# State products added up in memory by GpSimd transfers, and the weight stages' lower parts subtracted on GpSimd

## The chip, the core and the metric

The kernel runs on one core of one Trainium2 chip. The metric is the device time of one execution in microseconds (us). The core's engines work side by side, each through its own list of instructions in order, and wait for each other through semaphores: TensorE (PE, with weight loads as PEld), VectorE (DVE), ScalarE (ACT), GpSimd (POOL) and SyncE (SP), which here only issues transfers. Matrix results are in PSUM banks of 128 x 512 float32.

## What is computed

A decoder layer of three parts, each with a residual and a layer norm: differential attention, a state-space scan over a context, and a mixture of 16 experts. The change touches the first two, which one loop computes together.

```python
q, k, v = split(hidden @ Wqkv.T + b)                 # 16 q heads and 8 k heads of 128, v in pairs
p = softmax(q1 k1) - lam * softmax(q2 k2)            # causal
o = (p @ v) * rms * subln_w * (1 - LAMBDA_INIT)
x = layernorm(x + o.reshape(B, S, 2048) @ out_w.T + out_b)
...
def step(state, inp):                                # 4 batches, 512 channels, 16 states, 512 steps
    d, b, c, u = inp
    state = state * exp(d * A) + (d * u) * b
    return state, einsum('bdn,bn->bd', state, c)     # sum over the 16 states
y = (y + D * u) * silu(x)
```

## The kernel before

Matrix products are made from split operands: a value is a high part (rounded to the fp32r type) and a lower part (the value less the high part), and `three` (L602) issues three products hi*hi, hi*lo, lo*hi. So each weight and each result is cut in two: ScalarE writes the high part, and another engine subtracts for the lower part.

The main loop, `attend_and_scan`, has 64 passes p (and 2 that drain it) on each engine, in an order written out by hand. Each pass has two halves. In it the attention's work for one block m of 128 rows and one group g of heads goes through TensorE: scores of two units, turns of the probabilities, two projections (`project`, which run 7 ahead of their pass by AHEAD), values, turned heads, and `project_out(p-2)`. Sixteen passes are one group g, and there are 4 groups; four passes are one batch of a group. The x operand of the projections is reloaded from memory every four passes (`load_x`, L713 to L715) into the one buffer that there is.

Beside it runs the scan: in each pass one of 64 states (4 batches x 16), in two halves of 128 x 1024. For half k, k = 0 to 127: GpSimd's `drive(k)` writes dt*u*B into a slot of the ring `st` (4 slots); ScalarE's `decay` and VectorE's `scan` run twice over it; GpSimd then gates it (times C, L1279) and adds it into `y_sb` (L1284), and does `drive(k + 3)`. After a batch's 16 states, two transfers on GpSimd's own queue add `y_sb` to `scratch_y` in memory (L1291). So GpSimd has three operations in each half pass, and k is also the number of the half pass.

Weights come in stages of 128 x 512, 12 for each group: 8 of Wqkv (c = 0 to 7, called W stages here) and 4 of out_w (c = 8 to 11, called out stages). SP loads one into one of two slots of `w_stage`; `stage_high` on ScalarE writes the high part with the factor (the score scale, or the subln column) put on; `stage_low` on VectorE computes stage * factor - high. SP loads stage n + 2 into the slot when stage_lo says that stage n is done (L619), in its place in SP's list. `W_AT` places the W stages of the next group at half passes 19 to 24, 26 and 27 of a group. Two out stages are at the end of pass p % 16 == 1, before `proj_high` and the scan there, and two in the first half of pass p % 16 == 2, before the scan there. TensorE waits for them in two places: `project` (L769) and the first `project_out` of a group (L844), which comes in the first half of pass p % 16 == 2, just behind the scores.

When the loop is over, the expert phase begins: GpSimd adds `outb` to the first x (L1616), VectorE takes statistics of that and adds the last attention block (L1153) behind them, ScalarE waits for this block's transfer and for the scan's last sums.

Of the kernel before, what the change touches and what calls it, by code (L numbers as in the profile page):

```python
# [21 lines left out]
ALU = mybir.AluOpType  # L22
# [478 lines left out]
NB = 2  # L501
NSTAGE = 12
# [34 lines left out]
def attend_and_scan(nc, d, s, ctx, place, banks, early):  # L537
# [35 lines left out]
    y = sb("y_sb", [P, CT, T])  # L573
# [7 lines left out]
    def proj_bank(r):  # L581
# [7 lines left out]
             "stage_hi", "stage_lo", "vb_loaded", "vb_hi", "vb_lo", "xa_loaded", "xb_loaded",  # L589
# [4 lines left out]
             "dt_loaded0", "dt_loaded1", "dtu_loaded0", "dtu_loaded1", "y_added0", "y_added1",  # L594
             "b_loaded0", "b_loaded1", "c_loaded0", "c_loaded1",
             "dA_done", "dbu_done", "scan_done", "gated", "piece_done")
# [14 lines left out]
    def half(buf, h):  # L611
        return buf[:, 2 * h:2 * h + 2, :].rearrange("p c t -> p (c t)")

# [72 lines left out]
    def sync(sp, F):  # L686
# [65 lines left out]
        for h in range(2):  # L752
            sp.wait_ge(S[f"acc_stored{h}"], 16 * NM // 2)
            sp.wait_ge(S[f"y_added{h}"], 16 * B)
# [125 lines left out]
    def scalar(act, F, stages=None, blocks=()):  # L880
        def stage_high(n):

            g, c = divmod(n, NSTAGE)
            act.wait_ge(S[f"stage_loaded{n % 2}"], 16 * (n // 2 + 1))
            if c < 8:
                if g > 0:
                    act.wait_ge(S["proj_done"], 8 * (4 * g - 1) + (1, 1, 2, 3, 4, 5, 7, 7)[c] + 1)
                nc.scalar.activation(w[0][:, :, TILE_COL[c]:TILE_COL[c] + HD],
                                     stage[:, n % 2, :].rearrange("p (k n) -> p k n", k=KT), ACT.Copy,
                                     scale=SCALE if 2 <= c < 6 else 1.0).then_inc(S["stage_hi"], 1)  # L890
            else:
                t = c - 8
                act.wait_ge(S["subln_scaled"], 1)
# [161 lines left out]
    def vector(dve, F, stages=None, blocks=()):  # L1055
        def stage_low(n):

            g, c = divmod(n, NSTAGE)
            dve.wait_ge(S["stage_hi"], n + 1)
            raw = stage[:, n % 2, :]  # L1060
            if c < 8:
                cut = slice(TILE_COL[c], TILE_COL[c] + HD)
                nc.vector.scalar_tensor_tensor(w[1][:, :, cut], raw.rearrange("p (k n) -> p k n", k=KT),
                                               SCALE if 2 <= c < 6 else 1.0, f32(w[0][:, :, cut]),
                                               ALU.mult, ALU.subtract).then_inc(S["stage_lo"], 1)
            else:
                t = c - 8
                nc.vector.scalar_tensor_tensor(ow[1][:, t, :], raw, subln[:, t % 2:t % 2 + 1],
# [112 lines left out]
        for p in range(NM + 2):  # L1181
# [9 lines left out]
            if 2 * p in W_AT:  # L1191
                stage_low(W_AT[2 * p])
# [1011 lines left out]
```

## Time and profile before

| | |
|---|---|
| median of 3 runs | 1639.57 us (1638.88 to 1640.35) |
| the profiled execution | 1641.0 us, with a span of 1638.9 us |
| busy: PE, DVE, ACT, POOL | 1425.3, 1304.8, 1044.7, 1232.5 us |
| main loop | about 178 to 1149 us of the span |
| transfers, hardware queue (SP's) | 188.36 MB |
| transfers, GpSimd's queue | 4.19 MB |

The profile shows one execution. A row of the timeline has an instruction's start, its duration, its place in the code, tiles, and in brackets the idle time of its engine just before it and the instruction that ended it. The duration of one that stands behind another on the same engine can hold some waiting for that other, so the distance between two starts tells the pace. PEclk is the granted share of TensorE's full clock: 1.00 is 2.4 GHz and 0.50 is 1.2 GHz.

### The profile page before, as it was taken

How to read it: one execution, taken by the hardware profiler on the slowest of the kernel's cores; microseconds unless marked ns; L12 is line 12 of the kernel's file. 1: busy time of each engine (PE TensorE's matmuls, PEld its weight loads, DVE VectorE, ACT ScalarE, POOL GpSimd, SP SyncE). 2: the span in 40 equal slices, each digit the busy share in tenths (PEclk: the TensorE clock that was granted, in tenths of full speed). 3: DMA queues.
4: the chain of work that ended last, by engine and by line, in shares of the span. 5: the costliest groups of instructions: out<-in, count | busy, mean ns of one | idle time of the engine just before them, and what ended most of it. 6: DMA issues, size and time to landing. Idle time of an engine off the chain costs nothing.

```text
span 1638.9 us, 23260 instructions
## 1 busy us (share of the span) xinstructions
PE 1425.3 (87%) x7632; PEld 1145.2 (70%) x7632; DVE 1304.8 (80%) x2375; ACT 1044.7 (64%) x2407; POOL 1232.5 (75%) x613
## 2 busy tenths in 40 slices
PE   4646799999999999999999999986478999998996
PEld 1213678877888887888887788875366676676784
DVE  4998688899888899888899889886638668487575
ACT  3887557666666666666666566664457657577474
POOL 1346489999899999899999899999567347176263
PEclk8767889999999999999999999999699999998998
DMA  5484433453642443632453532325352032121021
GB/s 174 161 293 184 161 95 106 129 152 101 188 124 87 136 146 124 174 112 83 142 155 117 173 116 78 126 76 155 96 155 75 23 101 78 41 79 65 27 71 58
DMA packets 121664, 194.03 MB, mean 118 GB/s; under 512 B 10740, under 2 KB 60408, under 8 KB 120008
## 3 DMA queue, kind: packets, MB, share of 16 engines
q1 hardware_dynamic: 120392, 188.36, 35.7%
q0 software_dynamic: 1152, 4.19, 1.5%
q8 instruction: 60, 0.98, 0.2%
q14 instruction: 60, 0.49, 0.1%
HBM read 145.99 MB, written 46.53 MB: 117 GB/s over the span
## 4 chain that ended last, share of the span: by engine, by line
PE 41%; DVE 20%; POOL 16%; issue 12%; ACT 6%; DMA 2%; SPq 0%; POOLq 0%; DVEq 0%; ACTq 0%
PE banks L604 10%; PE banks L605 9%; PE banks L606 9%; POOL act_buf L1939 6%; DVE state L1160 4%; POOL state L1279 3%; POOL state L1253 3%; PE banks L1481 2%; PE banks L1482 2%; PE banks L1483 2%; DVE banks L1997 1%; PE banks L814 1%; POOL x_work L1616 1%; DVE banks L452 1%; DVE negmax L1100 1%
## 5 line engine op out<-in xcount | busy, mean ns | idle before, releaser
L1279 POOL TENSOR_TENSOR state<-state,Cn 128x1024 f32<-128x1024 f32 x120 | 292.6, 2438 | 47.8 <-DVE state L1160 47.5
L1160 DVE TENSOR_TENSOR_SCAN state<-banks,state 128x512 f32<-128x512 f32 x256 | 310.9, 1214 | 4.7 <-ACT banks L984 2.2
L1253 POOL TENSOR_TENSOR state<-dtu_sb,Bn 128x1024 f32<-128x1024 f32 x128 | 311.1, 2431 | 1.5 <-DMA Bn<-scratch_bc 1.4
L1939 POOL TENSOR_TENSOR act_buf<-act_buf,wb 128x512 f32<-128x512 f32 x128 | 165.8, 1297 | 172.5 <-ACT act_buf L1839 170.5
L1284 POOL TENSOR_TENSOR y_sb<-y_sb,state 128x1024 f32<-128x1024 f32 x120 | 287.2, 2393 | 9.4
L984 ACT ACTIVATE banks<-dt_sb,negA 128x512 f32<-128x512 f32 x256 | 177.4, 693 | 106.7 <-DVE state L1160 105.8
L604 PE MATMUL banks<-x_hi,w_hi 128*128 128x512 f32 (+1 forms) x512 | 189.4, 370 | 31.6 <-DVE qT_lo L1090 14.7
L606 PE MATMUL banks<-x_hi,w_lo 128*128 128x512 f32 (+1 forms) x512 | 179.4, 350 | 0.0
L605 PE MATMUL banks<-x_lo,w_hi 128*128 128x512 f32 (+1 forms) x512 | 179.2, 350 | 0.0
L604 PEld LDWEIGHTS banks<-x_hi,w_hi 128*128 128x128 f32 x512 | 101.7, 199 | 51.9 <-DVE qT_lo L1090 18.7
L1987 DVE TENSOR_TENSOR hid_lo<-banks,hid_hi 128x512 fp32r<-128x512 f32 x136 | 93.7, 689 | 53.9 <-ACT hid_hi L1851 51.8
L1997 DVE TENSOR_TENSOR banks<-banks,act_buf 128x512 f32<-128x512 f32 x136 | 94.4, 694 | 49.3 <-POOL act_buf L1939 25.6
L1100 DVE TENSOR_REDUCE negmax<-banks 128x2 f32<-128x512 f32 (+3 forms) x128 | 103.8, 811 | 20.1 <-PE banks L806 20.1
L1851 ACT CAST hid_hi<-banks 128x512 fp32r<-128x512 f32 x136 | 79.4, 584 | 61.3 <-DVE banks L1997 49.8
L606 PEld LDWEIGHTS banks<-x_hi,w_lo 128*128 128x128 f32 x512 | 101.6, 198 | 12.3
L605 PEld LDWEIGHTS banks<-x_lo,w_hi 128*128 128x128 f32 x512 | 102.2, 200 | 9.2
L604 PE MATMUL banks<-ow_hi,hT_hi 128*128 128x512 f32 x256 | 106.2, 415 | 1.5 <-DVE hT_lo L1146 1.4
L1481 PE MATMUL banks<-xl_hi,cw_hi 128*128 128x512 f32 x256 | 102.4, 400 | 3.0 <-ACT act_buf L1837 2.9
L930 ACT ACTIVATE prob<-banks,negmax 128x256 f32<-128x256 f32 (+3 forms) x128 | 67.4, 527 | 57.3 <-DVE negmax L1100 55.7
L1837 ACT ACTIVATE act_buf<-banks 128x512 f32<-128x512 f32 x136 | 81.6, 600 | 33.0 <-PE banks L1483 27.9
L1482 PE MATMUL banks<-xl_lo,cw_hi 128*128 128x512 f32 x256 | 101.5, 397 | 0.0
L1483 PE MATMUL banks<-xl_hi,cw_lo 128*128 128x512 f32 x256 | 101.5, 397 | 0.0
(219 smaller groups left out, 4448.9 us busy)
## 6 DMA issues: line engine op xcount, KB each, us to landing
x_hi<-scratch_xs SPq DMA_DIRECT2D x32, 512.0 KB, 5.0
x_lo<-scratch_xs SPq DMA_DIRECT2D x32, 512.0 KB, 6.3
Cn<-scratch_bc SPq DMA_DIRECT2D x64, 256.0 KB, 3.4
Bn<-scratch_bc SPq DMA_DIRECT2D x64, 256.0 KB, 3.9
scratch_acc<-acc_sb SPq DMA_DIRECT2D x64, 256.0 KB, 2.1
wb<-scratch_wT SPq DMA_DIRECT2D x64, 256.0 KB, 3.2
acc_sb<-scratch_acc SPq DMA_DIRECT2D x48, 256.0 KB, 3.1
w_stage<-in_w SPq DMA_DIRECT2D x32, 256.0 KB, 3.3
```

The lines of the kernel that those rows point to most:

```text
L604: nc.tensor.matmul(out, at_l(lhs[0]), at_r(rhs[0]), start=start, stop=False)
L605: nc.tensor.matmul(out, at_l(lhs[0]), at_r(rhs[1]), start=False, stop=False)
L606: return nc.tensor.matmul(out, at_l(lhs[1]), at_r(rhs[0]), start=False, stop=stop)
L984: nc.scalar.activation(dA[:, :], dt[:, ct, :], ACT.Exp, scale=s["negA"][:, ct * NS + state:ct * NS + state + 1]) \
L1160: nc.vector.tensor_tensor_scan(row, dA[:, :], row, 0.0, ALU.mult, ALU.add) \
L1253: nc.gpsimd.tensor_tensor(st[:, k % 4], dtu[:, 2 * h:2 * h + 2, :], Bn[:, state % NB, :].unsqueeze(1).broadcast_to([P, 2, T]), ALU.mult).t ...
L1279: nc.gpsimd.tensor_tensor(to, st[:, k % 4], Cn[:, state % NB, :].unsqueeze(1).broadcast_to([P, 2, T]), ALU.mult).then_inc(S["gated"], 1)
L1284: nc.gpsimd.tensor_tensor(y[:, 2 * h:2 * h + 2, :], y[:, 2 * h:2 * h + 2, :], st[:, k % 4], ALU.add).then_inc(S["piece_done"], 1)
L1481: nc.tensor.matmul(out, at_l(lhs[0]), at_r(rhs[0]), start=start, stop=False)
L1482: nc.tensor.matmul(out, at_l(lhs[0]), at_r(rhs[1]), start=False, stop=False)
L1483: return nc.tensor.matmul(out, at_l(lhs[1]), at_r(rhs[0]), start=False, stop=stop)
L1939: nc.gpsimd.tensor_tensor(act_[:, N % 3, :], act_[:, N % 3, :], wb[:, E % 3, :], ALU.mult) \
```

## The change

The sum y in on-chip memory and its adds are gone. Each gated half state, 128 x 1024, is itself added to `scratch_y` by a transfer on GpSimd's queue: 128 of them, where there were 8. Two transfers to the same half of y must not be in flight together, so each waits for the one two half passes earlier, and the ring has 6 slots, so that a slot is free again when its transfer has landed. The `stage_low` of the first 8 stages stays on VectorE; the 40 others go to GpSimd, as a plain subtraction. For that, ScalarE first scales the stage in its slot, waits for itself, and then writes the high part: two operations for each of these 40 stages, where there was one. The places in ScalarE's list are the old ones. On GpSimd they follow the gate and the drive of the same half pass.

```diff
@@ attend_and_scan
-    y = sb("y_sb", [P, CT, T])
+    st_more = sb("state_more", [P, 2, 2, T])
+    def ring(k):
+        at = k % RING
+        return st[:, at] if at < 4 else st_more[:, at - 4]
+
+    def stage_scale(c):
+        return SCALE if 2 <= c < 6 else 1.0 if c < 8 else subln[:, c % 2:c % 2 + 1]
@@ scalar: stage_high
             act.wait_ge(S[f"stage_loaded{n % 2}"], 16 * (n // 2 + 1))
+            raw = stage[:, n % 2, :]
+            if n >= 8:
+                act.wait_ge(S["subln_scaled"], 1)
+                nc.scalar.activation(raw, raw, ACT.Copy,
+                                     scale=stage_scale(c)).then_inc(S["stage_scaled"], 1)
+                act.wait_ge(S["stage_scaled"], n - 7)
...
-                nc.scalar.activation(ow[0][:, t, :], stage[:, n % 2, :], ACT.Copy,
-                                     scale=subln[:, t % 2:t % 2 + 1]).then_inc(S["stage_hi"], 1)
+                nc.scalar.activation(ow[0][:, t, :], raw, ACT.Copy).then_inc(S["stage_hi"], 1)
@@ vector: the loop
-            if 2 * p in W_AT:
-                stage_low(W_AT[2 * p])
-            if p % 16 == 2 and p < NM:
-                stage_low(NSTAGE * (p // 16) + 10)
-                stage_low(NSTAGE * (p // 16) + 11)
...
-            if p % 16 == 1 and p < NM:
-                stage_low(NSTAGE * (p // 16) + 8)
-                stage_low(NSTAGE * (p // 16) + 9)
...
-            if 2 * p + 1 in W_AT:
-                stage_low(W_AT[2 * p + 1])
@@ gpsimd
+        def wait_added(k):
+            state, h = divmod(k, 2)
+            pool.wait_ge(S[f"y_added{h}{state % 2}"], 16 * (state // 2 + 1))
@@ gpsimd: drive
+            if k >= RING:
+                wait_added(k - RING)
+            nc.gpsimd.tensor_tensor(ring(k), dtu[:, 2 * h:2 * h + 2, :],
                                     Bn[:, state % NB, :].unsqueeze(1).broadcast_to([P, 2, T]),
                                     ALU.mult).then_inc(S["dbu_done"], 1)
@@ gpsimd: new
+        def stage_low(n):
+            g, c = divmod(n, NSTAGE)
+            if n == 8:
+                pool.wait_ge(S["stage_lo"], 8)
+            pool.wait_ge(S["stage_hi"], n + 1)
+            raw = stage[:, n % 2, :]
+            if c < 8:
+                cut = slice(TILE_COL[c], TILE_COL[c] + HD)
+                nc.gpsimd.tensor_tensor(w[1][:, :, cut], raw.rearrange("p (k n) -> p k n", k=KT),
+                                        f32(w[0][:, :, cut]), ALU.subtract).then_inc(S["stage_lo"], 1)
+            else:
+                nc.gpsimd.tensor_tensor(ow[1][:, c - 8, :], raw, f32(ow[0][:, c - 8, :]), ALU.subtract) \
+                    .then_inc(S["stage_lo"], 1)
@@ gpsimd: the loop
+            nc.gpsimd.tensor_tensor(ring(k), ring(k),
                                     Cn[:, state % NB, :].unsqueeze(1).broadcast_to([P, 2, T]),
                                     ALU.mult).then_inc(S["gated"], 1)
-            if r > 0:
-                pool.wait_ge(S["gated"], k + 1)
-                nc.gpsimd.tensor_tensor(y[:, 2 * h:2 * h + 2, :], y[:, 2 * h:2 * h + 2, :],
-                                        st[:, k % 4], ALU.add).then_inc(S["piece_done"], 1)
             if k + 3 < NDRIVE:
                 drive(k + 3)
-            if r == NS - 1:
-                pool.wait_ge(S["piece_done"], added(k))
-                nc.gpsimd.dma_start(d["y"][b][:, 2 * h * T:2 * (h + 1) * T], half(y, h), accum_op=ALU.add) \
-                    .then_inc(S[f"y_added{h}"], 16)
+            if k in W_AT:
+                stage_low(W_AT[k])
+            if k % 32 in (3, 4):
+                for c in range(2):
+                    stage_low(NSTAGE * (k // 32) + 2 * (k % 32 + 1) + c)
+            pool.wait_ge(S["gated"], k + 1)
+            if r > 0:
+                wait_added(k - 2)
+            nc.gpsimd.dma_start(d["y"][b][:, 2 * h * T:2 * (h + 1) * T],
+                                ring(k).rearrange("p c t -> p (c t)"), accum_op=ALU.add) \
+                .then_inc(S[f"y_added{h}{state % 2}"], 16)
```

The expert phase's waits for y_added are spread over the four new semaphores in the same way.

GpSimd's list at half passes 35 and 36 (pass 17's second half and pass 18's first, where the second group's out stages are), before:

```order
L1279 TENSOR_TENSOR state<-state,Cn 128x1024 [waits c_loaded1,scan_done]
L1284 TENSOR_TENSOR y_sb<-y_sb,state 128x1024 [waits gated]
L1253 TENSOR_TENSOR state<-dtu_sb,Bn 128x1024 [waits piece_done,b_loaded1]
L1279 TENSOR_TENSOR state<-state,Cn 128x1024 [waits c_loaded0,scan_done]
L1284 TENSOR_TENSOR y_sb<-y_sb,state 128x1024 [waits gated]
L1253 TENSOR_TENSOR state<-dtu_sb,Bn 128x1024 [waits piece_done,b_loaded1]
```

The same two half passes on GpSimd now:

```order
L1283 TENSOR_TENSOR state_more<-state_more,Cn 128x1024 [waits c_loaded1,scan_done]
L1248 TENSOR_TENSOR state<-dtu_sb,Bn 128x1024 [waits y_added00,b_loaded1]
L1264 TENSOR_TENSOR ow_lo<-w_stage,ow_hi 128x512 [waits stage_hi] x2
L1296 DMA scratch_y<-state_more 128x1024 [waits y_added10,gated]
L1283 TENSOR_TENSOR state<-state,Cn 128x1024 [waits c_loaded0,scan_done]
L1248 TENSOR_TENSOR state<-dtu_sb,Bn 128x1024 [waits y_added10,b_loaded1]
L1264 TENSOR_TENSOR ow_lo<-w_stage,ow_hi 128x512 [waits stage_hi] x2
```

The add has gone, a transfer stands last, and the four subtractions of the out stages stand behind gate and drive; the second pair is behind the gate that waits for pass 18's second scan.

VectorE's list in the same place, from the end of pass 17 to the second scan of pass 18 (qT_lo is a projection's lower part, L1160 the scan), before:

```order
L1121 TENSOR_TENSOR pT_lo<-banks,pT_hi 128x384 [waits pt_hi]
L1068 SCALAR_TENSOR_TENSOR ow_lo<-w_stage,subln,ow_hi 128x512 [waits stage_hi] x2
L1160 SCALAR_TENSOR_TENSOR state<-banks,state 128x512 [waits dbu_done,dA_done]
L1090 SCALAR_TENSOR_TENSOR qT_lo<-banks,qk_bias,qT_hi 128x512 [waits proj_hi]
L1146 TENSOR_TENSOR hT_lo<-banks,hT_hi 128x512 [waits ot_hi]
L1100 TENSOR_REDUCE negmax<-banks 128x2 [waits scores_done]
L1121 TENSOR_TENSOR pT_lo<-banks,pT_hi 128x384 [waits pt_hi]
L1160 SCALAR_TENSOR_TENSOR state<-banks,state 128x512 [waits dbu_done,dA_done]
...
L1090 SCALAR_TENSOR_TENSOR qT_lo<-banks,qk_bias,qT_hi 128x512 [waits proj_hi]
L1068 SCALAR_TENSOR_TENSOR ow_lo<-w_stage,subln,ow_hi 128x512 [waits stage_hi] x2
L1160 SCALAR_TENSOR_TENSOR state<-banks,state 128x512 [waits dbu_done,dA_done]
```

On VectorE the two rows of L1068 are gone now and nothing takes their place, so each scan follows the row above it.

## Rows read from the trace of the kernel before

**Rows 1.** Windows: stretch, its length, busy time (count) of each engine, PEclk, DMA

```profile
980.00:1090.00 110.00, 109.96 (x696) 94.42 (x696) 94.28 (x187) 72.70 (x203) 108.69 (x47) 1.00 0.30 97
320.00:430.00 110.00, 104.55 (x629) 88.41 (x628) 101.20 (x183) 71.14 (x200) 103.89 (x45) 0.97 0.48 144
```

**Rows 2.** Timeline, VectorE: one attention block's add of four passes

```profile
322.35 0.68 DVE L1153 TENSOR_TENSOR acc_sb<-banks,acc_sb 128x512 f32<-128x512 f32 x1
...
415.35 0.68 DVE L1153 TENSOR_TENSOR acc_sb<-banks,acc_sb 128x512 f32<-128x512 f32 x1
...
993.12 0.68 DVE L1153 TENSOR_TENSOR acc_sb<-banks,acc_sb 128x512 f32<-128x512 f32 x1
...
1076.99 0.68 DVE L1153 TENSOR_TENSOR acc_sb<-banks,acc_sb 128x512 f32<-128x512 f32 x1
```

**Rows 3.** Timelines of VectorE and TensorE around the second group's out stages

```profile
446.74 2.56 DVE L1068 SCALAR_TENSOR_TENSOR ow_lo<-w_stage,subln,ow_hi 128x512 fp32r<-128x512 f32 x1 [0.33 <-ACT ow_hi L896]
451.79 0.80 PE L604 MATMUL banks<-x_hi,w_hi 128*128 128x512 f32 x1 [3.50 <-DVE qT_lo L1090]
458.70 1.40 DVE L1068 SCALAR_TENSOR_TENSOR ow_lo<-w_stage,subln,ow_hi 128x512 fp32r<-128x512 f32 x2
460.02 1.22 DVE L1160 TENSOR_TENSOR_SCAN state<-banks,state 128x512 f32<-128x512 f32 x1
460.25 0.47 PE L604 MATMUL banks<-ow_hi,hT_hi 128*128 128x512 f32 x1
```

**Rows 4.** Windows, as rows 1: behind TensorE's wait of 3.50 us

```profile
452.00:456.00 4.00, 4.00 (x10) 3.13 (x11) 2.93 (x7) 1.72 (x6) 3.92 (x3) 0.50 0.52 164
```

**Rows 5.** The tile w_stage: ScalarE's instructions, durations ns min/median/max, first and last start

```profile
L888 ACT ACTIVATE w_hi<-w_stage x32: 613/632/651, 22.9 to 872.3; 128x512 fp32r<-128x512 f32 x32
...
L896 ACT ACTIVATE ow_hi<-w_stage,subln x16: 710/715/722, 203.2 to 943.3; 128x512 fp32r<-128x512 f32 x16
```

**Rows 6.** Timeline, GpSimd: the loop's last half passes and what follows them

```profile
1125.60 2.34 POOL L1279 TENSOR_TENSOR state<-state,Cn 128x1024 f32<-128x1024 f32 x1
1128.02 2.35 POOL L1284 TENSOR_TENSOR y_sb<-y_sb,state 128x1024 f32<-128x1024 f32 x1
1130.33 2.36 POOL L1279 TENSOR_TENSOR state<-state,Cn 128x1024 f32<-128x1024 f32 x1
...
1135.45 0.88 POOL L1291 DMA_DIRECT2D scratch_y<-y_sb  x1 [0.30 <-POOL y_sb L1284]
1136.07 2.68 POOL L1279 TENSOR_TENSOR state<-state,Cn 128x1024 f32<-128x1024 f32 x1
...
1142.08 5.23 POOL L1616 TENSOR_TENSOR x_work<-x_work,outb 128x512 f32<-128x512 f32 x4
```

**Rows 7.** Timelines of VectorE, SP and TensorE: the x load in a W stage

```profile
354.31 1.21 DVE L1160 TENSOR_TENSOR_SCAN state<-banks,state 128x512 f32<-128x512 f32 x1
...
359.33 0.63 SPq L637 DMA_DIRECT2D x_lo<-scratch_xs  x1
...
368.29 0.37 PE L604 MATMUL banks<-x_hi,w_hi 128*128 128x256 f32 x1
```

**Rows 8.** The tile x_lo between 355 and 363 us: landing of its two loads

```profile
DMA to landing us min/median/max: 6.6/6.9/7.2
```

**Rows 9.** Timelines of VectorE and TensorE, end of the loop

```profile
1125.74 1.22 DVE L1160 TENSOR_TENSOR_SCAN state<-banks,state 128x512 f32<-128x512 f32 x1 [1.88 <-POOL state L1253]
...
1139.96 0.69 DVE L1146 TENSOR_TENSOR hT_lo<-banks,hT_hi 128x512 fp32r<-128x512 f32 x1 [1.44 <-ACT hT_hi L975]
1143.70 0.69 DVE L1582 BATCH_NORM_STATS2 stats<-x_work 128x6 f32<-128x512 f32 x1 [3.04 <-POOL x_work L1616]
...
1148.43 0.69 DVE L1153 TENSOR_TENSOR acc_sb<-banks,acc_sb 128x512 f32<-128x512 f32 x1
```

**Rows 10.** The page's queues (packets, MB, share of 16 engines) and issues (count, KB, landing us)

```profile
q0 software_dynamic: 1152, 4.19, 1.5%
...
scratch_y<-y_sb POOLq DMA_DIRECT2D x8, 512.0 KB, 6.9
```

More of the change, by code:

```diff
@@ L501 @@
 NB = 2
+RING = 6
 NSTAGE = 12
@@ L593, in attend_and_scan @@
              "acc_loaded0", "acc_loaded1", "acc_stored0", "acc_stored1",
-             "dt_loaded0", "dt_loaded1", "dtu_loaded0", "dtu_loaded1", "y_added0", "y_added1",
+             "dt_loaded0", "dt_loaded1", "dtu_loaded0", "dtu_loaded1", "y_added00", "y_added01", "y_added10", "y_added11",
              "b_loaded0", "b_loaded1", "c_loaded0", "c_loaded1",
-             "dA_done", "dbu_done", "scan_done", "gated", "piece_done")
+             "dA_done", "dbu_done", "scan_done", "gated")
     S = {n: ctx.enter_context(nc.semaphore(n)) for n in names}
@@ L753, in sync @@
             sp.wait_ge(S[f"acc_stored{h}"], 16 * NM // 2)
-            sp.wait_ge(S[f"y_added{h}"], 16 * B)
+            for odd in range(2):
+                sp.wait_ge(S[f"y_added{h}{odd}"], 16 * NSTATE // 2)
     def tensor(pe, F, blocks=None):
@@ L888, in stage_high @@
                 nc.scalar.activation(w[0][:, :, TILE_COL[c]:TILE_COL[c] + HD],
-                                     stage[:, n % 2, :].rearrange("p (k n) -> p k n", k=KT), ACT.Copy,
-                                     scale=SCALE if 2 <= c < 6 else 1.0).then_inc(S["stage_hi"], 1)
+                                     raw.rearrange("p (k n) -> p k n", k=KT), ACT.Copy,
+                                     scale=stage_scale(c) if n < 8 else 1.0).then_inc(S["stage_hi"], 1)
             else:
                 t = c - 8
-                act.wait_ge(S["subln_scaled"], 1)
                 if g > 0:
                     act.wait_ge(S["out_done"], 16 * g)
-                nc.scalar.activation(ow[0][:, t, :], stage[:, n % 2, :], ACT.Copy,
-                                     scale=subln[:, t % 2:t % 2 + 1]).then_inc(S["stage_hi"], 1)
+                nc.scalar.activation(ow[0][:, t, :], raw, ACT.Copy).then_inc(S["stage_hi"], 1)
         def vb_high(g):
@@ L1056, in stage_low @@
         def stage_low(n):
-            g, c = divmod(n, NSTAGE)
             dve.wait_ge(S["stage_hi"], n + 1)
[L1060 to L1068, printed above, removed]
-                                               f32(ow[0][:, t, :]), ALU.mult, ALU.subtract) \
-                    .then_inc(S["stage_lo"], 1)
+            cut = slice(TILE_COL[n], TILE_COL[n] + HD)
+            nc.vector.scalar_tensor_tensor(w[1][:, :, cut], stage[:, n % 2, :].rearrange("p (k n) -> p k n", k=KT),
+                                           stage_scale(n), f32(w[0][:, :, cut]),
+                                           ALU.mult, ALU.subtract).then_inc(S["stage_lo"], 1)
         def vb_low(g):
@@ L1158, in scan @@
             dve.wait_ge(S["dbu_done"], i // 2 + 1)
-            row = st[:, i // 2 % 4, i % 2, :]
+            row = ring(i // 2)[:, i % 2, :]
             nc.vector.tensor_tensor_scan(row, dA[:, :], row, 0.0, ALU.mult, ALU.add) \
@@ L1677, in first_loads @@
         for h in range(2):
-            sp.wait_ge(A[f"y_added{h}"], 16)
+            for odd in range(2):
+                sp.wait_ge(A[f"y_added{h}{odd}"], 16 * NS // 2)
         load_y(sp, 0)
@@ L1868, in scalar @@
         for n in range(2):
-            act.wait_ge(A[f"y_added{n}"], 16 * B)
+            for odd in range(2):
+                act.wait_ge(A[f"y_added{n}{odd}"], 16 * NSTATE // 2)
         for n in range(2):
```

16 lines of the change are left out of this document (1 added, 15 removed).

## The prediction

> **What bounds the kernel now.** I read the windows first. In plain passes (980 to 1090 us) TensorE is busy for 109.96 of 110 us at full clock, and GpSimd for 108.69 [rows 1]. So both are full, and the question is who ends last. In the passes with W stages (320 to 430 us) TensorE is busy for 104.55 of 110 at a granted clock of 0.97, so something makes it wait. The distance of attention blocks says how much that is: the same six passes take 83.87 us in a plain place (993.12 to 1076.99) and 93.00 us with the W stages of the second group in them (322.35 to 415.35) [rows 2]. I take this excess of 9.1 us for each of the three times that W stages are loaded in the loop, 27 us.
>
> The timelines tell its cause: VectorE. The first of the out stages' lower parts takes 2.56 us on it, where two together take 1.40 us at 458.70, while GpSimd happens to be idle. Scan, projection and heads queue up behind, and TensorE waits 3.50 us, until 451.79 [rows 3]. After that its granted clock is 0.50 (1.2 GHz), with 10 matmuls in 4 us [rows 4], so about 0.40 us each, of which full clock would give back 0.20.
>
> GpSimd is nearly full, but it holds up little: only at the loop's end does VectorE's scan wait for it (1.88 us at 1125.74) [rows 9]. Its three operations of a half pass cost 2.42 + 2.31 us and as much as the latter for the drive (1125.60, 1128.02, 1130.33), 7.1 us in all [rows 6], beside 83.87 / 12 = 7.0 us that TensorE needs here. **So taking 2.4 us from GpSimd frees an engine that is not last in most of the loop**. What the change can win is the 27 us of the W stages, a like stall at the out stages, and the loop's end.
>
> **GpSimd's new half pass.** The add goes (120 times). A transfer comes: at 1135.45 it starts 0.30 us after the add's end, and the next gate, 2.68 instead of some 2.4 us long, has really begun at about 1136.35, so it costs 1.2 us of GpSimd [rows 6]. Gate 2.35, drive 2.35 and transfer 1.2 make 5.9 us. A lower part of 128x512 on GpSimd is like L1616, 5.23 / 4 = 1.3 us [rows 6]: 7.2 us in a half pass with a W stage. That is the pace of TensorE, so GpSimd keeps up, now with slack in plain passes. The wait for the transfer of two half passes earlier is 14 us behind it, and such a transfer lands in 6.9 us [rows 10]: nothing. A ring of 6 is wide enough for the same reason.
>
> **ScalarE** does one operation more for 40 stages, 0.63 to 0.72 us [rows 5], plus some 0.15 us of waiting for itself. At W stages it lies mostly in waits of ScalarE for VectorE, which was late there; I leave 0.5 us a group for it. At the out stages two of them stand before `proj_high`, for which TensorE waits: 1.65 us.
>
> **Out stages, the main cost.** There are four such places, one a group. At the end of pass 17 VectorE loses 3.14 us of lower parts (446.74 to 449.88, when the scan behind them starts) and ScalarE adds 1.65 us, so TensorE restarts about 1.4 us earlier than 451.79. But the second pair is in pass 18. Before, it stood on VectorE before the second scan, was done at 460.02, and TensorE began the group's first `project_out` at 460.25 with hardly a wait [rows 3]. Now it stands on GpSimd behind gate(36) and drive(39), and gate(36) waits for that very scan. The scan starts at 460.02 - 1.32 (the pair in front of it) - 1.4 - some 0.5 (the half clock after a shorter wait is shorter) = 456.8 and ends 1.1 later, 457.9. Then 0.1 + 2.35 + 2.35 + 2 x 1.3 = 7.4 us make 465.3. **TensorE, with nothing to do since about 458, starts `project_out` at 465.4 in place of 460.25, 5.1 us later.** It comes out of a wait of 7 us, so its 12 matmuls run at half clock, 12 x 0.20 = 2.4 us more. Everything behind is bound by TensorE, so nothing is given back. A group costs 7.5 us, four cost **+30.0 us**. Bounds: 3.5 a group (no clock loss, GpSimd early by 1.5) to 9.5 (the loads of the pair, which wait for the first pair on GpSimd, late by 2): +14 to +38.
>
> **W stages.** The 9.1 us go with VectorE's lower parts, but a new wait comes. SP's list has, in pass 11's second half, the load of a stage that waits for the lower part of half pass 23, and behind it the load of x for the projections of pass 12. Before, x_lo was issued at 359.33, 3.9 us after pass 11's last scan had ended (354.31 + 1.13), and was used at 368.29, 12.9 us after it [rows 7]. With GpSimd about 1.0 us behind, gate 2.4, drive 2.35 and lower part 1.3 end 7.05 us after the scan; a stage, an acc and the x_hi load go before, 1.9 us; x_lo is issued at 9.0 and lands 6.6 to 7.2 us later [rows 8], at 15.9. TensorE waits 3.0 to 3.4 us and pays half clock for some 1.8 more. With ScalarE's 0.5 and VectorE's v bias part, which stays (0.5), 6.2 of 9.1 us are left: 2.9 x 3 = **-8.7 us**. Bounds: 0 to -27, from a wait as long as the old one to none.
>
> **The end.** The scan's wait of 1.88 us goes. The last hT_lo, at 1139.96, comes to 1138.1. The statistics waited for GpSimd's x_work, which began at 1142.08 after the last transfer; GpSimd is now through with its loop some 9 us earlier (last gate and transfer, 3.6 us after the last scan), so they start at 1138.8 and take 3.7 us of work. The last block's add comes at 1142.5 instead of 1148.43 [rows 9]: **-5.9 us** (-4 to -8).
>
> **Sum.** 30.0 - 8.7 - 5.9 = +15.4 us. On the profiled execution's 1641.0 us this is 1656.4; the median of the runs is 1.4 below, so 1655.0.
>
> **A page that speaks against the change.** The transfer's issue is priced at 1.2 us by the row at 1135.45, where VectorE was not in such an operation. The Trainium skill, SBUF — State Buffer, section SBUF: two separate sides, says that GpSimd cannot write a transfer's descriptors while VectorE runs an operation in a two-port mode. No row here shows it; the third rival has it as a mechanism.
>
> **Rivals.** *First, not slower:* the x load comes in time and the out stages cost only their 5.1 us. The point is whether x_lo lands within 12.9 us of the scan, so is issued by 6. For it speaks that SP's queue was in time before by 2.1 us; against it, the 7.05 us to the lower part, each of which is a row. It gives -27 - 5.9 + 20.4 = -12.5: 1627.1 us. If there is also no clock loss and the lower parts come early, 1620.
>
> *Second, transfers in each other's way.* Eight such transfers took 1.5% of the span of all 16 engines [rows 10], 3.1 us each, 128 take 0.43 of the loop on top of the 0.30 to 0.48 there [rows 1]. If each of the 15 x loads lands 3.1 us later, it is 1.0 us past its use by the margin there [rows 7, 8], and with 1.5 us of half clock this is 15 x 2.5 = 38 us more: 1693. Against it: the margin is greater in plain passes, and the queues are not full on average. The Trainium skill, DMA: Bandwidth & Descriptors, section Issuing engines are not separate DMA queues, says that all queues share the 16 engines; its sum for a transfer of this size would be 3.2 us, where the row has 6.9.
>
> *Third, GpSimd stays the bound*, because a transfer costs it more than the row says while VectorE works. From 2.3 us a transfer on, its half pass is longer than TensorE's 7.0; at 2.6 it is 0.3 x 128 = 38 us in place of the W stages' gain, 1680 to 1700. Then the change doesn't do what it says.
>
> **Chances.** Forecast 0.50, first rival 0.25, second 0.13, third 0.12. What a measurement can't tell from no change is 0.2%, 3.3 us. Of the forecast 0.05 lies within it, and of the first rival 0.05; the rest of the first, 0.20, is faster, all else, 0.70, slower. The forecast's own range is 1641 to 1672. 8 times in 10 the time should be between 1625 and 1686, which takes in most of the first rival and the lower part of the last two.
>
> **What would show it.** Right: TensorE's first `project_out` of each group, four times, behind a wait of 6 to 9 us that ends on GpSimd's ow_lo, and a PEclk of 0.50 after it; the wait of 3.50 us down to about 2; the x matmuls of passes 12, 28 and 44 behind a wait for a transfer; VectorE's last L1153 about 6 us nearer to its last scan; GpSimd under 88% busy in plain passes, whose six passes still take 84 us. Wrong: no wait at `project_out`; plain passes longer than 84 us (second or third rival, told apart by GpSimd's busy share); no wait for x (first).

## The result and the profile after

The changed kernel takes 1718.24 us (median of 4 runs, 1710.75 to 1726.39), the kernel before 1639.64: a ratio of 1.048, interval 1.045 to 1.050. It is slower by 78.6 us where the prediction had 15.4, outside its range of 1625 to 1686. The profiled execution was the longest of the four; its span of 1724.6 us is 85.7 more than the 1638.9 of before, and the sums below are made against that.

The same two spans of six passes as in [rows 2], then windows (stretch, length, busy time and count of each engine, PEclk, DMA share, GB/s) of a plain place and of the second group's W stages, as [rows 1]:

```profile
330.40 0.68 DVE L1159 TENSOR_TENSOR acc_sb<-banks,acc_sb 128x512 f32<-128x512 f32 x1
...
434.63 0.68 DVE L1159 TENSOR_TENSOR acc_sb<-banks,acc_sb 128x512 f32<-128x512 f32 x1
...
1079.02 0.68 DVE L1159 TENSOR_TENSOR acc_sb<-banks,acc_sb 128x512 f32<-128x512 f32 x1
...
1162.91 0.68 DVE L1159 TENSOR_TENSOR acc_sb<-banks,acc_sb 128x512 f32<-128x512 f32 x1
```

```profile
1070.00:1150.00 80.00, 79.96 (x501) 68.89 (x499) 70.41 (x145) 54.11 (x155) 62.91 (x34) 1.00 0.81 175
340.00:450.00 110.00, 92.53 (x556) 78.56 (x554) 77.64 (x159) 66.34 (x183) 74.31 (x43) 0.92 0.67 171
```

Plain passes are what they were: 83.89 us for six, TensorE full, GpSimd down from 99% to 79% busy, although the DMA engines are now busy for 0.81 in place of 0.30. The six passes with W stages take 104.2 in place of 93.0 us. So the loss is in places. TensorE's longest waits between 200 and 1180 us (us in total, times, longest) are of three kinds:

```profile
PE banks L605 <- issue: 42.7, 3, 15.5
PE banks L605 <- POOL ow_lo L1264: 30.6, 4, 8.3
PE banks L605 <- DMA x_lo<-scratch_xs: 18.6, 3, 9.9
```

Where the view names "issue", it shows no releaser; these three are the first x matmuls of passes 12, 28 and 44, and each starts within 0.2 us of the landing of x_lo, so I read them as waits for x.

To sum the losses I take the distances of the blocks' adds (L1159, numbered from 0) less those in plain places (14.67, 15.48, 14.45, 12.29 us for number mod 4 = 1, 2, 3, 0). The sum of this **excess** over the places, with what lies behind the loop, is the whole difference. In the first group the out stages come before block 0's add, so there the later start of this add counts as theirs (6.5 us):

| place, blocks | before | after | difference | predicted |
|---|---|---|---|---|
| W stages, 8 to 13, 24 to 29, 40 to 45 | 26.5 | 59.1 | +32.6 | -8.7 |
| batch change, 15, 31, 47 | 0.0 | 25.8 | +25.8 | not in the sum |
| out stages, four groups | | | +27.4 | +30.0 |
| end of the loop, 58 to 63 | -15.4 | -17.3 | -1.9 | -5.9 |
| behind the loop | | | +1.7 | 0 |

The batch change is the pass at which the scan goes to its next batch and SyncE loads new halves of dt and dtu, three times in the loop.

**W stages.** Pass 11's last scan on VectorE and the first x matmul of pass 12 on TensorE, then SyncE's DMAs and GpSimd around them, in the W stages of the second group (start, length, idle before and what ended it):

```profile
360.01 1.21 DVE L1166 TENSOR_TENSOR_SCAN state_more<-banks,state_more 128x512 f32<-128x512 f32 x1
...
390.10 0.55 PE L605 MATMUL banks<-x_hi,w_hi 128*128 128x256 f32 x1 [15.54 <-issue]
```

```profile
365.85 0.55 SPq L630 DMA_DIRECT2D w_stage<-in_w  x1
366.44 0.62 SPq L659 DMA_DIRECT2D Cn<-scratch_bc  x1
367.10 0.48 SPq L705 DMA_DIRECT2D scratch_acc<-acc_sb  x1
367.63 0.90 SPq L654 DMA_DIRECT2D Bn<-scratch_bc  x1
379.89 0.55 SPq L630 DMA_DIRECT2D w_stage<-in_w  x1
380.48 0.62 SPq L700 DMA_DIRECT2D acc_sb<-in_x  x1
381.14 0.53 SPq L645 DMA_DIRECT2D x_hi<-scratch_xs  x1
381.72 0.89 SPq L645 DMA_DIRECT2D x_lo<-scratch_xs  x1
```

```profile
355.39 2.39 POOL L1248 TENSOR_TENSOR state<-dtu_sb,Bn 128x1024 f32<-128x1024 f32 x1 [5.35 <-DMA Bn<-scratch_bc]
357.75 1.29 POOL L1261 TENSOR_TENSOR w_lo<-w_stage,w_hi 128x512 fp32r<-128x512 f32 x1
...
364.28 1.54 POOL L1261 TENSOR_TENSOR w_lo<-w_stage,w_hi 128x512 fp32r<-128x512 f32 x1
365.51 1.15 POOL L1296 DMA_DIRECT2D scratch_y<-state_more  x1
366.12 2.95 POOL L1283 TENSOR_TENSOR state_more<-state_more,Cn 128x1024 f32<-128x1024 f32 x1
376.30 2.35 POOL L1248 TENSOR_TENSOR state<-dtu_sb,Bn 128x1024 f32<-128x1024 f32 x1 [7.23 <-DMA Bn<-scratch_bc]
378.60 1.26 POOL L1261 TENSOR_TENSOR w_lo<-w_stage,w_hi 128x512 fp32r<-128x512 f32 x1
```

The scan ended at 361.22. The x_lo load is issued at 381.72, 20.5 us later, where the prediction had 9.0 and before 3.8 [rows 7]. Read the rows as a ring. GpSimd's drive waits for B (7.23 us at 376.30). B was issued at 367.63, because it stands in SyncE's list behind the stage load of 365.85, which waited for the lower part that ends at 365.8. And this lower part stands on GpSimd behind a drive that had waited for B (5.35 us at 355.39). The next stage load, at 379.89, waits for the lower part of 378.60, and x stands behind it. So two half passes take some 20 us (355.39 to 376.30, drive to drive) in place of 14.

**Batch change.** SyncE, pass 13 to 16, with the last line of TensorE:

```profile
433.41 0.47 SPq L649 DMA_DIRECT2D dt_sb<-scratch_dt  x1
...
434.45 0.43 SPq L649 DMA_DIRECT2D dtu_sb<-scratch_dtu  x1
434.93 0.43 SPq L649 DMA_DIRECT2D dt_sb<-scratch_dt  x1
435.40 0.43 SPq L705 DMA_DIRECT2D scratch_acc<-acc_sb  x1
435.88 0.59 SPq L654 DMA_DIRECT2D Bn<-scratch_bc  x1
447.88 0.33 SPq L700 DMA_DIRECT2D acc_sb<-in_x  x1
448.26 0.53 SPq L645 DMA_DIRECT2D x_hi<-scratch_xs  x1
```

```profile
459.50 0.55 PE L605 MATMUL banks<-x_hi,w_hi 128*128 128x256 f32 x1 [9.86 <-DMA x_lo<-scratch_xs]
```

The acc load waits until the acc store of the same parity (issued at 435.40) has landed: 12.5 us, behind three loads of 512 KB that came together. In the kernel before these three were issued at 408.44, 410.18 and 414.46, and the store landed in 3.0 us.

**Out stages.** As predicted. GpSimd and TensorE in pass 18, where there was hardly a wait before [rows 3], and a window behind:

```profile
488.21 2.64 POOL L1283 TENSOR_TENSOR state<-state,Cn 128x1024 f32<-128x1024 f32 x1
490.51 2.62 POOL L1248 TENSOR_TENSOR state<-dtu_sb,Bn 128x1024 f32<-128x1024 f32 x1
492.81 2.75 POOL L1264 TENSOR_TENSOR ow_lo<-w_stage,ow_hi 128x512 fp32r<-128x512 f32 x2
```

```profile
495.71 0.77 PE L605 MATMUL banks<-ow_hi,hT_hi 128*128 128x512 f32 x1 [8.27 <-POOL ow_lo L1264]
```

```profile
496.00:499.00 3.00, 3.00 (x8) 2.33 (x8) 1.65 (x8) 0.85 (x2) 0.40 (x1) 0.50 0.76 83
```

Gate, drive and two lower parts, then TensorE at half clock: four such waits, 7.7 us on average. The wait of 3.50 us for the projection [rows 3] is down to 1.73.

### The profile page after: what moved, and what is told of

Same layout as the page of the kernel before. It is cut to its first block, busy times and chain, and to the rows that moved or that the text cites. A ratio compares the mean times of both kernels' runs of the same rounds, so it can differ in the third digit from the quotient of the medians.

```text
span 1724.6 us, 23458 instructions
## 1 busy us (share of the span) xinstructions
PE 1437.6 (83%) x7632; PEld 1156.0 (67%) x7632; DVE 1247.8 (72%) x2335; ACT 1067.4 (62%) x2447; POOL 1092.3 (63%) x653
## 4 chain that ended last, share of the span: by engine, by line
PE 28%; issue 25%; POOL 22%; DVE 11%; DMA 7%; ACT 4%; SPq 1%; POOLq 0%; DVEq 0%; ACTq 0%
PE banks L605 6%; PE banks L606 5%; PE banks L607 5%; POOL state L1283 5%; POOL act_buf L1947 5%; POOL scratch_y L1296 3%; DMA Bn<-scratch_bc 2%; PE banks L1487 2%; POOL state_more L1283 2%; PE banks L1488 2%; PE banks L1489 2%; DMA w_stage<-in_w 2%; POOL state L1248 1%; DMA scratch_acc<-acc_sb 1%; DVE banks L2005 1%
## 5 line engine op out<-in xcount | busy, mean ns | idle before, releaser
L1248 POOL TENSOR_TENSOR state<-dtu_sb,Bn 128x1024 f32<-128x1024 f32 x86 | 215.6, 2508 | 128.6 <-DMA Bn<-scratch_bc 117.7
L1283 POOL TENSOR_TENSOR state<-state,Cn 128x1024 f32<-128x1024 f32 x86 | 228.1, 2653 | 70.3 <-DVE state L1166 65.6
L1166 DVE TENSOR_TENSOR_SCAN state<-banks,state 128x512 f32<-128x512 f32 x172 | 209.0, 1215 | 1.9 <-ACT banks L998 1.5
L605 PEld LDWEIGHTS banks<-x_hi,w_hi 128*128 128x128 f32 x512 | 105.3, 206 | 106.6 <-issue 73.1
L1248 POOL TENSOR_TENSOR state_more<-dtu_sb,Bn 128x1024 f32<-128x1024 f32 x42 | 105.0, 2499 | 67.6 <-DMA Bn<-scratch_bc 62.8
L605 PE MATMUL banks<-ow_hi,hT_hi 128*128 128x512 f32 x256 | 110.9, 433 | 32.0 <-POOL ow_lo L1264 30.6
L1995 DVE TENSOR_TENSOR hid_lo<-banks,hid_hi 128x512 fp32r<-128x512 f32 x136 | 93.7, 689 | 54.3 <-ACT hid_hi L1858 52.4
L1283 POOL TENSOR_TENSOR state_more<-state_more,Cn 128x1024 f32<-128x1024 f32 x42 | 111.4, 2653 | 31.1 <-DVE state_more L1166 31.1
L607 PE MATMUL banks<-ow_hi,hT_lo 128*128 128x512 f32 x256 | 104.8, 409 | 0.0
L606 PE MATMUL banks<-ow_lo,hT_hi 128*128 128x512 f32 x256 | 104.5, 408 | 0.0
L1166 DVE TENSOR_TENSOR_SCAN state_more<-banks,state_more 128x512 f32<-128x512 f32 x84 | 102.0, 1215 | 1.2 <-ACT banks L998 1.1
```

What stands on the lines that cost most here:

```text
L605: nc.tensor.matmul(out, at_l(lhs[0]), at_r(rhs[0]), start=start, stop=False)
L606: nc.tensor.matmul(out, at_l(lhs[0]), at_r(rhs[1]), start=False, stop=False)
L607: return nc.tensor.matmul(out, at_l(lhs[1]), at_r(rhs[0]), start=False, stop=stop)
L1166: nc.vector.tensor_tensor_scan(row, dA[:, :], row, 0.0, ALU.mult, ALU.add) \
L1248: nc.gpsimd.tensor_tensor(ring(k), dtu[:, 2 * h:2 * h + 2, :], Bn[:, state % NB, :].unsqueeze(1).broadcast_to([P, 2, T]), ALU.mult).then_i ...
L1283: nc.gpsimd.tensor_tensor(ring(k), ring(k), Cn[:, state % NB, :].unsqueeze(1).broadcast_to([P, 2, T]), ALU.mult).then_inc(S["gated"], 1)
```

## The experiments

Theory one has three parts: the lower parts stand too late in GpSimd's half pass; SyncE's ordered list hands that on to the x loads; and at the W stages B closes the ring. Theory two: the 64 MB of accumulating transfers slow the loads. Theory three: GpSimd's own work is the bound. Each group of runs had the kernel before beside it, with a median of 1639.3 to 1640.7. In the table, us is the median of a kernel's runs. The other columns come from its one profiled execution, which can lie some us off the median: W, batch and out are the excess of the three W places, of the three batch changes (blocks 15, 31, 47) and of the last three out places. "x_lo" is the time from the end of pass 11's last scan to the issue of the first x_lo load of pass 12.

| kernel | us | W | batch | out | x_lo |
|---|---|---|---|---|---|
| before | 1639.6 | 26.5 | 0.0 | 18.6 | 3.8 |
| after | 1718.2 | 59.1 | 25.8 | 38.0 | 20.5 |
| x1_sp | 1678.3 | 33.4 | 12.7 | 37.6 | 11.8 |
| x2_pool | 1632.4 | 12.6 | 4.4 | 20.9 | 4.1 |
| x2b_out | 1691.3 | 58.5 | 18.8 | 19.3 | |
| x16_w_first | 1651.1 | 10.8 | 6.5 | 36.7 | |
| x3_dvelow | 1636.8 | 30.7 | 8.9 | 12.8 | 4.9 |
| x4_stages | 1716.0 | 54.3 | 0.0 | 57.3 | 18.4 |
| x13_addsfirst | 1655.7 | 26.5 | 0.0 | 31.5 | 10.7 |
| x6_bfirst | 1685.6 | 29.0 | 13.3 | 32.5 | 9.3 |
| x14_accpost | 1709.3 | 58.7 | 15.7 | 38.5 | |
| x15_last_two | 1706.2 | 62.9 | 10.8 | 37.7 | |
| x7_scale | 1645.7 | 29.9 | 1.7 | 16.3 | |
| x5_all | 1638.9 | 10.3 | 14.7 | 15.2 | |
| x9_best | 1625.5 | 15.0 | 0.0 | 22.3 | 3.3 |
| x10_acth | 1627.9 | 12.8 | 0.0 | 22.0 | |

### The transfers alone

x3_dvelow puts `stage_low`, with the factor, back on VectorE at its old places, and takes away GpSimd's calls of it and ScalarE's scaling operation. The accumulating transfers stay.

> The changed kernel with all lower parts of stages back on VectorE, where and as they stood before, and without ScalarE's operation more: the accumulating transfers alone. Theory one: the transfers cost nothing in the loop and give GpSimd's time at its end, so the kernel before less 6 us: 1634 (1628 to 1641). Theory two: loads landing 2 to 3 us later cost the x loads their margin: 1660 or more.

Measured: 1636.8 us, ratio 0.998 (0.996 to 1.001). The transfers alone are not the cause: the nine x loads in plain passes lose nothing. What they cost is 8.9 us at the batch changes and 4.2 us at the W stages, where x_lo landed up to 9.4 us after its issue and TensorE waited 2.5 us for it. About as much comes back at the out stages (18.6 to 12.8) and at the end.

### The lower parts on GpSimd alone

x4_stages brings `y_sb`, its 120 adds and eight transfers back and keeps the lower parts on GpSimd.

> The changed kernel with GpSimd's adds into y_sb and the ring of four as before, eight transfers in all: the lower parts on GpSimd alone. A half pass with a lower part is then 2.4 + 2.4 + 2.4 + 1.3 = 8.5 us on GpSimd beside TensorE's 7.0. Theory one: the stalls at the W stages and at project_out are there without any transfer, as large or larger: 1715 (1695 to 1740). Theory two: without the transfers nothing is late but project_out: 1665 (1655 to 1675).

Measured: 1716.0 us, 1.045 (1.044 to 1.047), with hardly a wait for B (15 us in all). The x_lo load is issued 18.4 us after the scan even so. The adds take the place of the waits in front of the lower parts: GpSimd's time ahead of a lower part matters, whatever fills it, and the ring through B is one way to fill it. Without accumulating transfers the batch changes cost nothing, though the lower parts are as late.

### The lower parts ahead of gate and drive

x2_pool moves the calls of `stage_low` on GpSimd, for W and out stages, in front of the gate of their half pass (before and after, cut):

```
         for k in range(NDRIVE):
             state, h = divmod(k, 2)
             b, r = divmod(state, NS)
+            if k in W_AT:
+                stage_low(W_AT[k])
+            if k % 32 in (3, 4):
+                for c in range(2):
+                    stage_low(NSTAGE * (k // 32) + 2 * (k % 32 + 1) + c)
             pool.wait_ge(S["scan_done"], 2 * k + 2)
...
-            if k in W_AT:
-                stage_low(W_AT[k])
-            if k % 32 in (3, 4):
...
```

> The changed kernel, with GpSimd's lower parts of the stages ahead of the gate and the drive of their half pass, not behind them. Theory one: the four waits of about 8.3 us at the first project_out fall to 2 or less, with the half clock behind them 8 to 10 us a group, 36 us; and a lower part no longer stands behind a drive that waits for B, so the loop between SyncE and GpSimd opens and most of the 15.3 us of the W stages goes as well, 30 us: 1652 (1640 to 1670). Theories two and three: GpSimd's work and the traffic are the same, only the four waits go: 1682 (1678 to 1690).

Measured: 1632.4 us, 86 less than the changed kernel and faster than before, 0.9935 (0.992 to 0.995). Theory one had foretold 1652 (1640 to 1670), so it had the direction and too little of it; theories two and three would have had 1682 for the same work and traffic. GpSimd and SyncE at the same place:

```profile
356.78 1.29 POOL L1261 TENSOR_TENSOR w_lo<-w_stage,w_hi 128x512 fp32r<-128x512 f32 x1
358.03 2.38 POOL L1288 TENSOR_TENSOR state_more<-state_more,Cn 128x1024 f32<-128x1024 f32 x1
...
358.09 0.55 SPq L630 DMA_DIRECT2D w_stage<-in_w  x1
...
360.13 0.63 SPq L645 DMA_DIRECT2D x_lo<-scratch_xs  x1
```

Pass 11's last scan ends at 356.1; the lower part now stands ahead of the gate that waits for this scan and of the drive, and x_lo is issued 4.1 us after the scan. GpSimd's waits for B are still there, 78 and 34 us by its two tiles, and no longer stand between the scan and the lower part.

x2b_out makes this move for the out stages alone, x16_w_first for the W stages alone.

> The changed kernel with the lower parts of the out stages alone ahead of gate and drive; those of the W stages stay behind them. If the two places are stalls of their own, only the four waits at project_out go, 6 us of excess with the half clock for each where the kernel with all lower parts ahead kept 6 of 12: 1718 - 24 = 1694 (1686 to 1700), and the W stages keep their 15.3 us. If the out stages hand the delay on from the W stages, or the other way round, 1665 or less.

> The changed kernel with the lower parts of the W stages alone ahead of gate and drive, those of the out stages behind them. With the out stages alone ahead it took 1691.3, 26.9 us less than the changed kernel, and with both 85.8 us less. If the two are stalls of their own, this one is 58.9 us below the changed kernel: 1659 (1653 to 1665), with 11 to 12 us of excess in the first block of each group and under 2 us in the 11th. If they feed each other, it is under 1650.

Measured: 1691.3 (1.032, 1.028 to 1.037) and 1651.1 (1.008, 1.005 to 1.010). The second is 8 us below its 1659 and 2 us outside its range of 1653 to 1665. The moves give 26.9 and 67.1 us, 94 together, where both at once give 86: nearly stalls of their own. Part of what they share is the batch change, which falls in both (25.8 to 18.8 and to 6.5).

x13_addsfirst is x4_stages with the lower parts ahead of gate, add and drive.

> The lower parts on GpSimd with its adds into y_sb as before (1716.0 us), and now these lower parts ahead of gate and drive. A half pass of 8.5 us on GpSimd stays. If the place of the lower parts is all that counts, this comes near the kernel with transfers and the lower parts ahead (1632): 1640. If GpSimd's own time counts as well, 8 half passes of the W stages at 1.5 us over TensorE's 7.0 are 12 us a group that its fullness in plain passes doesn't give back at once: 1660 (1650 to 1675).

Measured: 1655.7 us, so the place is not all that counts: it is worth 60 us there, and putting transfers in place of the adds another 23 (1655.7 to 1632.4), at W and out stages alike (26.5 to 12.6 and 31.5 to 20.9).

### SyncE's list

x1_sp moves the stage load of the even half pass behind the B load; x6_bfirst moves the B load to the head of the pass. GpSimd's order stays in both. The lines that x6_bfirst adds, and takes away further down:

```
+            if p + 2 < NSTATE:
+                sp.wait_ge(S["dbu_done"], 2 * p + 2)
+                load_b(sp, p + 2)
             if p < NM and p % 4 == 0 and p // 4 + 1 < IT:
```

> The changed kernel, with one move in SyncE's list alone: the load of the stage that waits for the even half pass's lower part stands behind that pass's C load, acc store and B load, not ahead of them. Theory one (SyncE's list: a stage load waits for GpSimd's lower part, the B load behind it comes late, GpSimd's drive waits for B, and its next lower part comes later still): the blocks' excess at the W stages, 15.3 us in the 11th block of three groups, falls to 5 or less, and the 6.7 to 12.1 us four blocks later, where SyncE issued acc, dt and dtu loads in a bunch, to about half. 30 + 13 us less: 1675 (1660 to 1688). Theory two (the 64 MB of accumulating transfers slow the loads): the traffic is the same, so 1710 or more. Theory three (GpSimd's own work is the bound): the same work, 1710 or more.

> The changed kernel with one move in SyncE's list: the B load for two states later stands at the pass's start, ahead of the x, stage, C and acc transfers. GpSimd's order is that of the changed kernel. The kernel with the lower parts ahead still had 112 us of GpSimd's waits for B and lost nothing by them; here the lower parts stand behind the drives. If those waits are what makes the lower parts late, they fall from 175 to under 60 us and the 15.3 us of the W stages to about 7; the four waits at project_out stay: 1688 (1678 to 1700). If the waits for B are only idle time that something else fills, 1710 or more.

Measured: 1678.3 (1.023, 1.020 to 1.025) and 1685.6 (1.029, 1.024 to 1.034). GpSimd's first waits of x6_bfirst, where those for B (175 us in the changed kernel) are gone:

```profile
POOL state L1283 <- DVE state L1166: 136.4, 61, 12.0
POOL state_more L1283 <- DVE state_more L1166: 78.9, 34, 12.2
POOL state L1248 <- issue: 10.5, 4, 4.7
```

With the ring open, x_lo is issued 9.3 us after the scan, which is the prediction's 9.0, and TensorE's wait is 6.41 us (15.54 in the changed kernel):

```profile
359.89 1.21 DVE L1166 TENSOR_TENSOR_SCAN state_more<-banks,state_more 128x512 f32<-128x512 f32 x1
...
370.37 0.80 SPq L645 DMA_DIRECT2D x_lo<-scratch_xs  x1
...
379.35 0.55 PE L605 MATMUL banks<-x_hi,w_hi 128*128 128x256 f32 x1 [6.41 <-issue]
```

This run is the prediction's own picture of the W stages, and it has 29.0 us of excess, in an execution that was the fastest of its five by 7 us: nothing of before's 26.5 is gained. The prediction had a wait of 3.0 to 3.4 us for an issue at 9.0. Here x_lo landed 8.9 us after its issue, not 6.6 to 7.2, and TensorE was ready for it 11.8 us after the scan, not 12.9.

### The batch change

x14_accpost puts the acc load behind the x loads of the next pass; x15_last_two puts only the lower parts of the last two W stages ahead.

> The changed kernel with one move in SyncE's list: the load of acc, which waits until the acc store of two passes earlier has landed, stands behind the x loads of the next pass, not ahead of them. In the changed kernel SyncE stood in that wait from 435.9 to 447.9 us, behind the dt and dtu loads, with the x loads of pass 16 behind it. If that wait makes them late, the 12.1, 6.7 and 7.0 us of the 15th, 31st and 47th block fall to 2 each, and the rest stays: 1718 - 20 = 1698 (1690 to 1706). If the x loads are late by the traffic itself, they still are: 1712 or more.

> The changed kernel with only the lower parts of the last two W stages of a group (GpSimd's half passes 26 and 27) ahead of gate and drive. The loads of the out stages in SyncE's list wait for these, and in the changed kernel the dt and dtu loads behind came in a bunch from 433.4 to 434.9 us. If the bunch makes the x loads of pass 16 late, through the acc store that lands behind it and the x loads in the same queue, the 12.1, 6.7 and 7.0 us of the 15th, 31st and 47th block fall to 9 us together, and the rest stays: 1701 (1694 to 1707). If it is the traffic of the accumulating transfers by itself, the three stay and it takes 1712 or more.

Measured: 1709.3 and 1706.2 us. x14_accpost gains 9 of the 20 us expected, and lies outside its range: x is issued from 435.56 on, some 12 us earlier, and its two x_lo loads land late all the same:

```profile
DMA to landing us min/median/max: 14.7/15.5/16.3
```

(10.5 to 13.8 in the changed kernel, 8.6 to 8.9 before.) In x15_last_two dt and dtu are issued at 427.50, 428.36 and 433.53, so the last of them no longer comes with the other two; the acc store lands in 6.0 us, and the batch changes fall from 25.8 to 10.8 (9 were expected). The DMA engines are full in that place in x15_last_two (last two columns: share, GB/s):

```profile
430.00:440.00 10.00, 10.00 (x71) 8.79 (x70) 9.39 (x19) 7.65 (x19) 7.00 (x5) 1.00 0.99 286
```

So 15 of the 26 us go with SyncE's list once more, and some 10 stay that come with the traffic, as in x3_dvelow (8.9). The two parts are not independent: x4_stages, with late lower parts and no such transfers, loses nothing here, and neither does x9_best below, with the transfers and the acc load moved.

### ScalarE's operation, and what beats both

x7_scale is x3_dvelow with ScalarE's scaling operation put back, 40 times.

> The accumulating transfers alone (1636.8 us), and ScalarE's operation more for 40 stages, with VectorE's lower parts as before but with a factor of 1. The prediction's price: 0.5 us a group at the W stages and 1.65 us in front of the projections at each of four out stages, 8 us in all: 1645 (1641 to 1650). If it lies in waits of ScalarE, 1637.

Measured: 1645.7 us, 8.9 more than x3_dvelow, where the prediction's terms for it add up to 8. Where they fall is not shown: the profiled execution of x7_scale was its fastest (1637.6), that of x3_dvelow was 1641.4, so their columns can't be set against each other.

x5_all joins the lower parts ahead with both moves in SyncE's list.

> The changed kernel with the lower parts ahead of gate and drive on GpSimd, the B load at the pass's start, and the stage loads of the even half pass behind the acc store. The kernel with the first alone has 1632.4. Its excess left is 3.7 us three times at the end of the W stages, 6.5 us four times at the out stages, 2 to 3 at the load of dt and dtu, and the loop's end. If SyncE's list still holds up the x loads, 1624 (1618 to 1629); if what is left is ScalarE's and VectorE's work there, 1632.

Measured: 1638.9 us (ratio 1.001, 0.998 to 1.004), a miss by 15 us. The W stages give 2 us more, but the batch changes take 14.7 us in place of 4.4, with TensorE waiting for x_lo's transfer. The waits for B that it removes cost nothing any more. At the three batch changes the first x_lo is issued as early as in x2_pool (15.6 to 17.2 us after the start of the pass's first scan, there 16.2 to 17.7), but it lands in 9.2 to 11.3 us in place of 7.0 to 7.7. The B load, 256 KB, is now issued just ahead of x; that it is the cause was not tested.

x9_best joins the lower parts ahead with the acc load behind the x loads, and leaves ScalarE's operation out where the factor is one; x10_acth puts `proj_high` ahead of the first two out stages on top.

```
-            if n >= 8:
+            if n >= 8 and 2 <= c < 6 or c >= 8:
...
                 load_x(sp, p // 4 + 1, 1)
+            if 3 <= p <= NM:
+                sp.wait_ge(S[f"acc_stored{(p - 1) % 2}"], 16 * ((p - 1) // 2))
+                load_acc(p - 1)
```

> The changed kernel with the lower parts ahead of gate and drive, the acc load behind the next pass's x loads, and without ScalarE's operation more at the four stages of a group whose factor is one. The first alone gave 1632.4. The acc load's place is worth what is left in the 15th, 31st and 47th block, 4.4 us, and part of the 43rd and 44th, 2 us; ScalarE's twelve operations less 1 us: 1625 (1618 to 1631).

> The kernel of the run before, and on ScalarE the projection's higher part ahead of the two stages at the out stages, not behind them. TensorE's wait of 1.5 us for that projection goes at four places, and the lower parts of ow come 0.7 us later, for which it waits 2 to 4 us: 3 us less at most: 1623 (1617 to 1630); if the later ow_lo costs as much as it gives, 1625.

Measured: 1625.5 (0.992, 0.989 to 0.995) and 1627.9 (0.992, 0.989 to 0.995): the same. The four waits for the projection (7.0 us) go, and the four for ow_lo grow from 11.0 to 19.5 us. x9_best is 15 us faster than the kernel before on the same chip. What stays is 22 us at the out stages, where TensorE still waits those 11 us for ow_lo, and 15 us at the W stages; no run takes these apart.

## Why the prediction was right or wrong

**What bounds.** Right: plain passes take 83.89 us again [rows 1, 2], GpSimd's relief of 20% wins nothing there.

**GpSimd's half pass.** Right for plain passes: 79% busy (under 88% foretold). "The wait for the transfer of two half passes earlier: nothing" held in the loop; at its end one such wait is 3.44 us.

**ScalarE.** Right in size: 8.9 us for the 8 (0.5 a group at the W stages, 1.65 at each of four out stages). Where they fall is not shown.

**Out stages.** Right in mechanism, place and size: waits of 7.7 us on average for 7, +27.4 us for +30.0.

**W stages.** The step that failed. The mechanism was named (x behind a stage load behind a lower part on GpSimd), but its size was worked out for one turn, with GpSimd "about 1.0 us behind" and a drive that waits for nothing. Measured from scan to x_lo, with the prediction's value in brackets: 4.9 us behind (1.0), gate 2.95 (2.4), wait for B 7.23 (0), drive and lower part 3.6 (3.65), SyncE's three loads 1.9 (1.9), in all 20.5 in place of 9.0. The prediction had followed SyncE's list up to the x load and left out the B load in it, whose reader is the very engine that the list waits for. A smaller part is the landing, 8.3 us for x_lo (6.6 to 7.2 [rows 8]). The difference is -8.7 to +32.6, 41 of the 70 us that were missing in the profiled execution. x6_bfirst shows that with 9.0 us right the term would still have been about +3, not -8.7, because x lands later and TensorE is ready for it earlier than the prediction had it. VectorE's relief doesn't show when x is last; where x is in time it does, as in x2_pool (26.5 to 12.6).

**The batch change** was in no term: 26 us. It is the same omission further down the list: stage loads that wait for GpSimd hold up the dt and dtu loads, which then come together, and the acc store's landing, late behind them, holds up x. x15_last_two shows 15 of these us.

**The end.** -1.9 for -5.9. The rows show two waits for loads there, which the prediction had not; that the transfers made them late was not tested:

```profile
1218.35 2.38 POOL L1283 TENSOR_TENSOR state<-state,Cn 128x1024 f32<-128x1024 f32 x1 [4.74 <-DMA Cn<-scratch_bc]
...
1224.02 0.69 DVE L1159 TENSOR_TENSOR acc_sb<-banks,acc_sb 128x512 f32<-128x512 f32 x1 [1.84 <-DMA acc_sb<-scratch_acc]
```

**The rivals.** The first (not slower) fell with the W stages. The second is wrong for plain passes; it holds at the batch changes, about 9 us, and at the W stages, about 4 (x3_dvelow), where it had 38. Its share of 0.43 for the transfers comes to 0.41 by its own rows (128 x 3.1 us in 971), and in plain passes the share rose by 0.51. The third is wrong: a transfer's issue holds GpSimd for 0.6 us between a lower part's end and the next gate (379.81 to 380.42), less than the 1.2 taken. By the Trainium skill, SBUF — State Buffer, section SBUF: two separate sides, GpSimd could have been locked out of these issues while VectorE runs an operation in a two-port mode. The trace doesn't tell which operations of VectorE run in one, so it doesn't test the rule; it shows no lock-out that counts, with 128 issues of 1.0 us in the mean and 1.8 at most.

**The range** was too narrow above because the W term's worst case was "a wait as long as the old one", that is no loss, and because the batch change was in no term. A new wait in a ring has no such bound.

## What to carry over

Work that moves to an engine with free time lands at a place in that engine's order, and the place can weigh more than the work: 86 us here for the same instructions, placed behind or ahead of two others. Where an in-order queue of loads waits for the engine that receives the new work, go down the whole queue past that wait, and ask for every load behind it who reads it; if the reader is the same engine, the delay feeds itself. Putting the moved piece ahead of the instructions that wait cost nothing here and opened the ring.

## What was not expected of the hardware

Accumulating transfers of 512 KB, 128 of them, raised the busy share of the DMA engines in plain passes from 0.30 to 0.81 and the landing of a B load from 3.9 to 6.9 us, and TensorE's passes did not get longer by 0.1 us. They cost time where 1.5 MB of loads came on top (share 0.96 to 0.99), and 4 us at the W stages.

In x9_best the first project_out of the four groups comes behind waits of 1.83, 1.84, 3.07 and 4.24 us, and the granted clock in the 2 us behind them reads 0.79, 0.77, 0.58 and 0.50 (third column from the end; the first and the last are shown):

```profile
217.20:219.20 2.00, 2.00 (x7) 1.61 (x8) 1.93 (x6) 1.56 (x7) 2.00 (x1) 0.79 0.00 0
...
936.30:938.30 2.00, 2.00 (x5) 1.61 (x6) 1.93 (x6) 1.57 (x7) 2.00 (x1) 0.50 0.16 31
```

0.50 is 1.2 GHz of 2.4. The length of the wait alone doesn't settle it: in the same execution the 2 us behind two waits of 1.77 and 1.78 us for a projection (until 926.06 and 446.79) read 1.00 and 0.55.
